# A fused three-layer kernel: one batch of expert blocks per step, results and stores in the first step, the reload of y moved behind one more step

## The reference

```python
x = x + (einsum('bsd,bdh->bsh', x, W[cat_ids]) + b[cat_ids][:, None, :])        # layer 0: y
h = gelu(einsum('bnd,hd->bnh', x, fc1_w) + fc1_b, approximate=False)            # fc1
shared = einsum('bnh,sh->bns', h, fc2_w) + fc2_b                                # fc2, 384 columns
expert = einsum('bnh,bph->bnp', h, experts_w[idx]) + experts_b[idx][:, None, :] # fc2, 128 columns
out = x + concatenate([shared, expert], axis=-1)
```

## Time and profile before

| | us |
|---|---|
| median of 3 runs | 1766.9 (1758.09 to 1769.2) |
| profiled execution, device time | 1764.9 |
| its span, first to last instruction | 1763.1 |
| PE busy | 1672.5 (95%) |
| PE weight loads busy | 1332.9 (76%) |
| DVE busy | 1161.8 (66%) |
| ACT busy | 548.3 (31%) |
| POOL busy | 188.8 (11%) |
| mean granted PE clock | 0.977 |

### The profile page before, as it was taken

How to read it: one execution, slowest core, us unless ns; L and a number is a source line. 1 busy time by engine, 2 the same in 40 slices (tenths; PEclk the granted TensorE clock), 3 DMA queues, 4 the chain that set the end, 5 groups by cost and what they waited for, 6 DMA issues and landing times.

```text
span 1763.1 us, 27990 instructions
## 1 busy us (share of the span) xinstructions
PE 1672.5 (95%) x7065; PEld 1332.9 (76%) x7065; DVE 1161.8 (66%) x2004; ACT 548.3 (31%) x927; POOL 188.8 (11%) x195
## 2 busy tenths in 40 slices
PE   7889999999999999999998999999999998999999
PEld 4678777777777777777776777778777776777787
DVE  4567666676666756677576667667677576676654
ACT  3333323232323323333233333323333232333321
POOL 0110100101010020200201001010100201002010
PEclk8999999999999999999999999999999999999999
DMA  6876676666766666666667666666666657666630
GB/s 185 171 175 143 138 152 139 125 133 150 145 144 128 133 148 132 158 145 126 145 115 159 140 139 137 134 152 146 146 141 124 152 122 160 142 126 149 122 76 25
DMA packets 884826, 243.44 MB, mean 138 GB/s; under 512 B 803688, under 2 KB 818168, under 8 KB 884732
## 3 DMA queue, kind: packets, MB, share of 16 engines
q1 hardware_dynamic: 740732, 203.75, 53.6%
q10 hardware_dynamic: 144000, 38.82, 10.0%
HBM read 209.93 MB, written 32.51 MB: 138 GB/s over the span
## 4 chain that ended last, share of the span: by engine, by line
PE 35%; SPq 30%; issue 13%; DMA 10%; DVE 5%; ACTq 4%; ACT 2%; POOL 0%; DVEq 0%; POOLq 0%
SPq L379 17%; PE ps_out L806 15%; PE ps_e L791 8%; PE ps_h L791 7%; DMA y_rows<-y 6%; PE ps_y L778 5%; SPq L334 5%; ACTq L519 4%; SPq L313 3%; DMA w_raw<-in_L_cond_W 2%; SPq L344 2%; ACT w_split L494 2%; DMA out<-resid 2%; DVE w_split L594 2%; DVE y L629 1%
## 5 line engine op out<-in xcount | busy, mean ns | idle before, releaser
L806 PE MATMUL ps_out<-w2e,h 128*128 128x512 f32 x3072 | 761.6, 396 | 15.0 <-DVE resid L669 14.8
L806 PEld LDWEIGHTS ps_out<-w2e,h 128*128 128x128 f32 x3072 | 574.5, 188 | 158.6 <-DVE resid L669 20.9
L791 PE MATMUL ps_e<-y_t,w 128*128 128x512 f32 x1536 | 387.1, 403 | 1.4 <-DVE y_t L594 1.4
L791 PE MATMUL ps_h<-y_t,w 128*128 128x512 f32 x1536 | 376.0, 394 | 0.0
L791 PEld LDWEIGHTS ps_e<-y_t,w 128*128 128x128 f32 x1536 | 299.6, 195 | 70.9 <-DVE y_t L594 1.8
L791 PEld LDWEIGHTS ps_h<-y_t,w 128*128 128x128 f32 x1536 | 288.6, 188 | 65.8
L525 ACT CAST w2e<-e_whole 128x512 fp32r<-128x512 f32 x256 | 158.4, 619 | 464.7 <-PE ps_out L806 200.1
L594 DVE TENSOR_TENSOR w_split<-w_raw,w_split 128x512 fp32r<-128x512 f32 x248 | 173.6, 735 | 144.5 <-ACT w_split L494 144.1
L778 PE MATMUL ps_y<-w_split,x_t 128*128 128x512 f32 x744 | 209.6, 419 | 49.6 <-DVE x_t L594 46.9
L494 ACT CAST w_split<-w_raw 128x512 fp32r<-128x512 f32 x248 | 146.2, 619 | 316.5 <-issue 165.6
L594 DVE TENSOR_TENSOR w2e<-e_whole,w2e 128x512 fp32r<-128x512 f32 x256 | 177.9, 695 | 65.9 <-ACT w2e L525 65.1
(11 more groups left out here) (63 smaller groups left out, 411.6 us busy)
## 6 DMA issues: line engine op xcount, KB each, us to landing
e_blocks<-in_L_cond_experts_w SPq DMA_DIRECT2D x1024, 64.0 KB, 2.8
w_raw<-in_L_cond_W SPq DMA_DIRECT2D x248, 256.0 KB, 2.7
out<-resid SPq DMA_DIRECT2D x64, 256.0 KB, 2.5
x_blocks<-in_x SPq DMA_DIRECT2D x240, 64.0 KB, 2.4
b_all<-in_L_cond_b SPq DMA_DIRECT2D x60, 256.0 KB, 4.2
x_raw<-in_x SPq DMA_DIRECT2D x60, 256.0 KB, 4.1
y_rows<-y ACTq DMA_DIRECT2D x60, 256.0 KB, 3.1
x_blocks<-y_rows ACTq DMA_DIRECT2D x240, 64.0 KB, 3.5
```

The source lines that it names most:

```text
L791: last = nc.tensor.matmul(h_bank(c)[:, :], w1[:, w, k, c * P:(c + 1) * P], y_t[:, a, k, :, :].rearrange("p b s -> p (b s)"), start=(k == 0 ...
L806: last = nc.tensor.matmul(ps_out[b][:, :], h[:, c % 2, a, b * S:(b + 1) * S], fc2_columns(c, c % 2, w, b), start=(c == 0 and n == 0), stop ...
```

## The change

In SP's stream, `load_experts` is called in every step for one batch (four DMAs), instead of in two steps of four for two batches each (eight DMAs). In step c it loads batch (c+1) mod 4 of quad (c+1)//4 + 1, so that a quad begins one step earlier than before, in the step before its former first one, and ends in the third after that. The first batch of quad 1 is issued in step 15 of the group before, ahead of the bias rows. `store` moves from step 2, ahead of that step's loads, to step 0, behind the loads of layer 0 and ahead of the expert blocks.

In ACT's stream, `store_y` is where it was. `load_y_blocks` is issued one step later than before, behind `e_high` and ahead of `gelu`.

In DVE's stream, all four `result` calls stand in step 0, behind `e_low` and ahead of `h_high`. In step 0 `turn_e` moves from in front of them to behind `h_low`.

```diff
--- before.py
+++ after.py
@@ -414,23 +414,23 @@
                 if j >= NC // 2:
                     for n in range(2 * j - NC, 2 * j - NC + 2):
                         load_experts(0, 0, first_experts, [n // (P // Q)], [n % (P // Q)])
+            load_experts(0, 1, first_experts, [0])
 
             def body(g, more):
                 idx = first_experts if first(g) else [index(exps, g * GB + b, exp_w.shape[0]) for b in range(GB)]
 
                 for c in range(NC):
-                    if c == 2 and not first(g):
-                        store(g - 1)
                     if more:
                         load_l0_in(g + 1, c)
-                    if c % QUAD in (0, 1):
-                        batches = range(2) if c % QUAD == 0 else range(2, GB)
-                        if c + QUAD < NC:
-                            load_experts(g, c // QUAD + 1, idx, batches)
-                        elif more:
-                            if c % QUAD == 0:
-                                next_idx = [index(exps, (g + 1) * GB + b, exp_w.shape[0]) for b in range(GB)]
-                            load_experts(g + 1, 0, next_idx, batches)
+                    if c == 0 and not first(g):
+                        store(g - 1)
+                    b, quad = (c + 1) % GB, (c + 1) // QUAD + 1
+                    if quad < NC // QUAD:
+                        load_experts(g, quad, idx, [b])
+                    elif more:
+                        if b == 0 and quad == NC // QUAD:
+                            next_idx = [index(exps, (g + 1) * GB + i, exp_w.shape[0]) for i in range(GB)]
+                        load_experts(g + 1, quad - NC // QUAD, next_idx, [b])
                     if first(g) and c == 0:
                         sp.dma_start(b2_all[:, :], fc2_b.rearrange("(o n) -> o n", o=1).to_broadcast([P, SHARED]))\
                           .then_inc(b2_in, 16)
@@ -572,15 +572,15 @@
                             w_high(g + 1, j)
                         for b in begun_in(c):
                             x_high(g + 1, b)
+                    e_high(g, c)
+                    if more:
                         for b in summed_in(c - 1):
                             store_y(g + 1, b)
-                    e_high(g, c)
+                        for b in summed_in(c - 2):
+                            load_y_blocks(g + 1, b)
                     gelu(g, c)
                     for n in range(PREP_RATE):
                         prep_high(prep_in_step(g, c, n))
-                    if more:
-                        for b in summed_in(c - 1):
-                            load_y_blocks(g + 1, b)
                 if more:
                     for b in range(GB):
                         y_high(g + 1, b)
@@ -636,6 +636,12 @@
                 after(dve, e_lo, g * NC + c)
                 off = (c % QUAD) * P
                 nc.vector.transpose(e_whole[:, :], e_blocks[:, (c // QUAD) % 2, :, off:off + P]).then_inc(e_turned, 1)
+
+            def turn_next_e(g, c, more):
+                if c + 1 < NC:
+                    turn_e(g, c + 1)
+                elif more:
+                    turn_e(g + 1, 0)
 
             def e_low(g, c):
                 after(dve, e_hi, g * NC + c + 1)
@@ -696,21 +702,18 @@
                         for b in begun_in(c):
                             x_low(g + 1, b)
 
-                    if c == 1 and not first(g):
-                        result(g - 1, 2)
-                        result(g - 1, 3)
                     copy_last(g, c)
                     e_low(g, c)
-                    if c + 1 < NC:
-                        turn_e(g, c + 1)
-                    elif more:
-                        turn_e(g + 1, 0)
                     if c == 0 and not first(g):
-                        result(g - 1, 0)
-                        result(g - 1, 1)
+                        for b in range(GB):
+                            result(g - 1, b)
+                    if c > 0:
+                        turn_next_e(g, c, more)
                     h_high(g, c)
                     prep_low(prep_in_step(g, c, 0))
                     h_low(g, c)
+                    if c == 0:
+                        turn_next_e(g, c, more)
                     prep_low(prep_in_step(g, c, 1))
                     if more:
                         if c == 0:
```

## The result

The changed kernel takes 1685.8 us (median of 4 runs, 1683.9 to 1688.6) against 1765.5 for the kernel before: ratio 0.9555, 95% interval 0.952 to 0.959, or 4.4% faster. 1707 was forecast, with 1684 to 1748 as the range; the time came out beside rival 2 (1686), which was given 0.14.

A forecast was written before the change was run, and what follows sets the result against it. PE's matmuls, busy 95% of the span, were taken as the bound. 1763.1 - 83.3 + 18 (step 1) + 4.5 (quad 1) + 1 (group 0) gave 1703.3 us of span, hence a 1707 us median; range 1684 to 1748.

The forecast's parts named there:

- rival 2: SP runs ahead: the extra batch at the group boundary is hidden and quad 1 is in time; 1686 us, chance 0.14.
- group 0: In the first group prep_high stands behind a slightly later gelu: 0 to +2 us in all, booked as +1.
- the new waits: Added PE waits: 18 us in step 1 for x's low part and 4.5 us for late quad 1.
- The 83.3 us to be won: PE's waits and half-clock matmuls, against 100.9 us for a group without waits; 5.6 us a group.
- Step 5: ACT waits for y's store to land before rounding W, making x's low part late; the 46.9 us of waits go.
- The reads in front of gelu: ACT's reads of y ahead of gelu: cost zero if hidden, up to 2.65 us four times a group if uncovered.
- rival 4: Steps 5, 9, 12, 14: reads ahead of gelu make every reload 2 us late on PE; 1827 us, chance 0.06.
- The boundary: SP's extra expert batch delays the first x blocks: a PE wait of 1.2 us a group in step 1, 18 us.
- Quad 1: Its expert blocks come late for turn_e(4), ahead of h(3): near the limit, 0.3 us a group, 4.5 us.
- The results: All four on DVE in step 0 cost zero, and fc2's first-step waits of 14.8 us go.
- Rival 3: ACT's and SP's DMA issues exclude each other, holding gelu 2.3 us more per reload of y; 1737 us, chance 0.03.
- Rivals 1 and 5: Half clock at each boundary, 1746 us, chance 0.22; step 5's wait only changes its cause, 1765 us, chance 0.05.

The follow-up runs named there:

- run 6: Changed kernel with the expert bias rows issued in step 12 instead of 15 and turn_e of a quad's first tile behind h_low: 1661.7 us, ratio 0.940.
- run 4: Changed kernel without ScalarE's part, that is with ScalarE's order of before: 1755.1 us, ratio 0.991.
- run 1: Kernel before with ScalarE's part alone (e_high ahead of store_y, reads of y one step later ahead of gelu): 1683.3 us, ratio 0.951.
- run 10: Changed kernel with the reads of y behind gelu in the same later step: 1704.8 us, ratio 0.962.
- run 9: Kernel before with the reads of y one step later but still behind gelu, store_y still ahead of e_high: 1732.4 us, ratio 0.980.
- run 2: Kernel before with only the expert blocks spread, one batch in every step, quad 1's first ahead of the boundary: 1749.7 us, ratio 0.990.
- Run 7: Changed kernel with only the bias rows of the next group's experts moved to step 12 from 15: 1662.7 us, ratio 0.938.
- run 5: Kernel before with ScalarE's and VectorE's parts, SP's stream wholly as before: 1675.9 us, ratio 0.949.

## Why the prediction was right in its way and short in its size

The sum of the forecast was 1703.3 us of span and 1682.1 were measured. With run 6 as the measure of a group almost without waits, the 21 us can be placed: 9 in the first term, 12 in group 0, none in the new waits.

**The 83.3 us to be won** rested on 100.9 us for a group without waits, taken from a group with three listed waits. Run 6 shows 100.26 on the mean and 100.1 without a wait. A wait costs PE some 0.25 us more than its idle time is listed with: that group took 103.53 us, 3.4 over 100.1, for three waits with 2.64 us listed. The blocks of six behind a wait take 1.65 instead of 1.54 us, which is part of it. So 1496.0 - 1403.7 = 92.3 us could be won in groups 1 to 14 as run 6 wins them, not 83.3.

**The new waits** were put at 18 + 4.5 = 22.5 us. Measured against run 6, the change has 1426.0 - 1403.7 = 22.3 us of them (17.5 listed). That the sum fits is luck: its first term was too high and its second too low, as told below.

**Step 5.** The cause was right: run 4 puts ACT's old order back and the wait is back with it, run 1 takes the new order alone and the wait is gone. The clock followed: it is 1.00 in the window over groups 1 to 14.

**The reads in front of gelu** were booked at zero with a price of 2.65 us uncovered, and rival 4 made them the way to a slower kernel. Wrong in its sign: run 10 shows that behind gelu they cost some 11 to 20 us more, and run 9 is 49 us over run 1 (1732.4 against 1683.3), through VectorE's transpose. The prediction had seen that DVE waits for the last read's landing, and called it nothing; with the reads in front it is nothing (about 81 us of DVE's waits for the read blocks, and no wait of PE behind them), one gelu later it is not. Rival 4's point of decision, y stored later than 29.1 us into the group, was nearly reached: 802.01 is 28.5, not the 26.5 of the sum, since quad 1 held the sum of y.

**Group 0** is the step that failed. The prediction let gelu come later there (0 to +2 us, booked as +1); group 0 got 11.0 us shorter. ACT's timeline of the changed kernel shows why the reads cost little:

```profile
83.70 0.62 ACT L494 CAST w_split<-w_raw 128x512 fp32r<-128x512 f32 x1
84.02 0.65 ACTq L519 DMA_DIRECT2D x_blocks<-y_rows  x1
84.23 0.62 ACT L494 CAST w_split<-w_raw 128x512 fp32r<-128x512 f32 x1
84.71 0.66 ACTq L519 DMA_DIRECT2D x_blocks<-y_rows  x1
84.75 0.61 ACT L500 CAST x_t<-x_whole_t 128x512 fp32r<-128x512 f32 x1
85.27 0.62 ACT L525 CAST w2e<-e_whole 128x512 fp32r<-128x512 f32 x1
85.39 1.34 ACTq L519 DMA_DIRECT2D x_blocks<-y_rows  x2
86.85 0.69 ACT L539 ACTIVATE g_raw<-ps_h,b 128x512 f32<-128x512 f32 x1 [0.96 <-issue]
```

The first three issues start while the four roundings that stand in front of them are still at work, and only the end of the last two sticks out; gelu is held for 0.96 us by issues that take 2.65 us. At the end of a step, with the engine empty and a landing to wait for, they cost their full time. Group 0 also prepares the weights of fc1 and fc2 behind each gelu, and PE's transposes wait for that: from 60 us on these waits are 9.7 us before and 2.7 in the changed kernel. Runs 9 and 10 bear it out from the other side: with the reads behind gelu group 1 starts at 182.9 us in the one and 172.9 in the other. The start of group 1 moves from 174.3 us to 165.9 with ScalarE's part (run 1), to 167.7 with the spread (run 2), to 168.3 with all but ScalarE's part (run 4), and to 163.3 with the whole change: two causes that overlap. With the spread VectorE's wait for expert blocks in group 0 falls from 4.6 to 0.6 us; that this is its part of the gain was not tried.

**The boundary** was right in mechanism and near in size. Counted were 3.8 us more work on SP, less 0.7: first x blocks 3.1 us later, measured 3.2; a wait of 1.2 us a group, measured 9.2 us listed, in twelve groups. Run 7 takes 2.0 us from that path and both it and the next wait vanish. **Quad 1** was put at 24.3 us to landing from the first x blocks, and `turn_e(4)` started 25.4 behind them: 0.3 us a group forecast, 8.3 us listed in thirteen. So of the two waits this one was put too low and the boundary's too high. The store of the results in step 0 did not bring y's store to 26.5 us either, for the same reason.

**The results**: the 14.8 us went. But that this part and the spread are each a gain was wrong. In the changed kernel what the results give is lost again through SP's two moves: without them (run 5) the ratio is 0.949 against 0.9555, and the waits in steps 1 and 3 are all but gone. ScalarE's part alone has the whole 4.4%.

**Rival 3** fell: ACT's four issues at 804.66 take 2.71 us within SP's bursts, as before. Rivals 1 and 5 did not come: the longest new wait, 1.59 us, left the clock at 1.00. Rival 2 gave the right time for a wrong reason: its boundary wait was to be hidden, and it wasn't. That the time fell inside the range at its lower end is owed to that rival's place in the range, not to a cause that had been seen.

## What to carry to other kernels

When several edits are made together, price each alone: here one of three carried the gain, and the other two passed their waits to each other through one in-order queue. On a loop boundary look for the queue that does its table reads and its jump there, and move what can go elsewhere, even four small DMAs: 2 us off that path gave 1.4% by the medians. A DMA that an engine's own stream issues costs least right behind work already handed to the engine, and costs most at a place where the engine is empty and a landing has to be waited for; then look at who reads what it brings, and when.

## What I had not expected of the hardware

ACT's queue issues DMAs while ACT computes what was given to it before: the first read is issued at 84.02 during the rounding of 83.70, ahead of three roundings that stand in front of it in the program, and four issues of 2.65 us in all held gelu for 0.96 us. And PE loses about 0.25 us more by a short wait at full clock than the timeline lists as idle, partly in the block behind it (1.65 against 1.54 us for six matmuls): run 6's groups with one wait of 0.55 us took 100.9 us, those without 100.1.
